# Window attention and a displaced blur on one core: who issues the stores of the residual and of the output, and in how many pieces the residual is read back

## The reference, cut to what matters

```python
x = x + window_attention(group_norm(x))   # 7x7 windows, 12 heads of 16, relative bias, projection
x = x + blur(group_norm(x))               # each channel shifted by a whole offset, then a 5x5 Gauss
```

## Time and profile before

| | |
|---|---|
| median of 3 runs | 5955.9 us (5952.99 to 5961.64) |
| the profiled execution's own time | 5947.59 us |
| its span | 5945.8 us |
| TensorE matmuls busy | 5372.8 us (90% of the span) |
| VectorE busy | 4278.6 us (72%) |
| ScalarE busy | 3798.7 us (64%) |
| GpSimd busy | 3556.2 us (60%) |
| mean granted TensorE clock | 0.936 |

### The profile page before, as it was taken

How to read it: one execution, slowest core, us unless ns; L and a number is a source line. 1 busy time by engine, 2 the same in 40 slices (tenths; PEclk the granted TensorE clock), 3 DMA queues, 4 the chain that set the end, 5 groups by cost and what they waited for, 6 DMA issues and landing times.

```text
span 5945.8 us, 259453 instructions
## 1 busy us (share of the span) xinstructions
PE 5372.8 (90%) x98232; PEld 4462.4 (75%) x98232; DVE 4278.6 (72%) x9682; ACT 3798.7 (64%) x8451; POOL 3556.2 (60%) x3940
## 2 busy tenths in 40 slices
PE   4998999999999999999999999999999999999996
PEld 3777777777777777777777777777777777777775
DVE  3777777777777777777777777777777777777773
ACT  1666666666666666667666666666666666666662
POOL 0566556666566666566665566665666655566664
PEclk9999999999999999999999999999999999999996
DMA  2566665666665666655666655666656666656653
GB/s 60 128 139 143 141 139 129 135 138 143 138 138 124 143 136 144 142 133 126 143 137 141 142 132 130 141 139 136 145 125 134 138 141 139 139 128 136 137 129 65
DMA packets 1353356, 790.32 MB, mean 133 GB/s; under 512 B 1187912, under 2 KB 1237512, under 8 KB 1344392
## 3 DMA queue, kind: packets, MB, share of 16 engines
q1 hardware_dynamic: 1352200, 774.03, 58.6%
HBM read 157.09 MB, written 154.14 MB: 52 GB/s over the span
## 4 chain that ended last, share of the span: by engine, by line
PE 37%; SPq 33%; issue 10%; ACT 8%; DVE 6%; DMA 5%; POOL 0%; ACTq 0%; DVEq 0%; POOLq 0%
SPq L414 13%; SPq L420 11%; PE pO L641 6%; SPq L432 5%; PE pT L624 3%; DMA xr<-x_scratch 2%; PE pS L598 2%; PE pS L590 2%; PE pM L509 2%; PE pT L617 2%; PE pT L608 2%; PE pM L511 2%; PE pM L510 1%; PE pO L651 1%; DMA kst<-mix 1%
## 5 line engine op out<-in xcount | busy, mean ns | idle before, releaser
L1222 POOL TENSOR_TENSOR probl<-prob,probh 98x588 f16<-98x588 f32 x1024 | 1332.2, 1301 | 398.3 <-DVE probh L1066 287.8
L1228 POOL TENSOR_TENSOR o<-osb,o 128x192 f16<-128x192 f32 x1024 | 598.6, 585 | 1434.0 <-ACT o L860 1414.9
L641 PEld LDWEIGHTS pO<-vv,probh 98*49 98x49 f16 x24576 | 866.2, 121 | 206.7 <-issue 151.6
L641 PE MATMUL pO<-vv,probh 98*49 98x34 f16 x24576 | 1017.7, 225 | 1.4 <-ACT om L868 1.2
L641 PE MATMUL pO<-vv,probl 98*49 98x34 f16 x12288 | 990.0, 228 | 2.3 <-issue 2.3
L852 ACT ACTIVATE mov<-pT 12x98 f16<-12x98 f32 x1024 | 244.6, 239 | 993.9 <-PE pT L608 992.7
L1051 DVE TENSOR_REDUCE mx<-pS 128x12 f32<-128x588 f32 x1024 | 776.7, 759 | 18.9 <-PE pS L598 6.1
L641 PEld LDWEIGHTS pO<-vv,probl 98*49 98x49 f16 x12288 | 765.9, 121 | 2.4 <-issue 2.4
L847 ACT ACTIVATE prob<-pT 98x588 f32<-98x588 f32 x1024 | 671.7, 656 | 147.0 <-PE pT L624 133.0
L624 PE MATMUL pT<-qst,kst 96*98 96x49 f16 x12288 | 750.8, 207 | 1.0 <-issue 0.8
L590 PE MATMUL pS<-biasT,addb 128*64 128x294 f16 x4096 | 617.5, 310 | 124.9 <-DMA kst<-mix 77.7
(11 more groups left out here) (192 smaller groups left out, 16086.5 us busy)
## 6 DMA issues: line engine op xcount, KB each, us to landing
kst<-kh SPq DMA_DIRECT2D x1536, 98.0 KB, 2.2
qst<-qh SPq DMA_DIRECT2D x1536, 49.0 KB, 2.4
qst<-mix SPq DMA_DIRECT2D x768, 98.0 KB, 2.6
kst<-mix SPq DMA_DIRECT2D x768, 98.0 KB, 2.5
vv<-cv SPq DMA_DIRECT2D x1024, 73.5 KB
xr<-x_scratch SPq DMA_DIRECT2D x64, 1176.0 KB
out<-xr SPq DMA_DIRECT2D x256, 294.0 KB
x_scratch<-xm SPq DMA_DIRECT2D x256, 196.0 KB, 3.2
```

What stands on the lines that cost most here:

```text
L641: mm = pe.matmul(pO[64 * win:64 * win + NT, OW * hp:OW * hp + OW], b[0:98, p % 2, PW * hp + NT * win:PW * hp + NT * win + NT], vv[:, g % 2 ...
L1222: pool.tensor_tensor(probl[0:98, p % 2, :], prob[0:98, p % 2, :], probh[0:98, p % 2, :], ALU.subtract).then_inc(S["pl_p"], 1)
L1228: pool.tensor_tensor(o16[:, p % 2, C:2 * C], osb[:, p % 2, :], o16[:, p % 2, 0:C], ALU.subtract).then_inc(S["ol_p"], 1)
```

## The change

The stores leave SP and go to ACT, where they stand behind the exponential of a step, two transfers in a step: chunk 0 of x1 at steps 16 and 17, chunk 1 at 24 and 25, chunk 2 at 0 and 1, chunk 3 at 6 and 7 of the next body (first the two from `xm`, then the two from `xt`); the output's quarters at 19, 23, 27 and 31 as before. The stores of chunk 3 count on a semaphore of their own. SP reads the residual back in four transfers of 24 channel places each, over all 112 partitions (588 KB each), at steps 6, 10, 12 and 14, and GpSimd waits for one quarter before every fourth multiplication. Before the first store of a new image, at step 16, ACT waits for all four quarters.

```diff
+READS = (6, 10, 12, 14)
...
-            def read_x1(s):
-
-                sp.dma_start(xr[HW * s:HW * s + HW, :],
-                             scratch[s].rearrange("y c x -> y (c x)")).then_inc(S["xr_in"], 16)
+            def read_x1(i, n):
+
+                cols = slice(CC // 4 * n, CC // 4 * n + CC // 4)
+                sp.dma_start(xr[0:SY, CC // 4 * HW * n:CC // 4 * HW * (n + 1)],
+                             scratch[:, :, cols].rearrange("s y c x -> (s y) (c x)")).then_inc(S[f"xr_in{n}"], 16)
...
-                    if p % PPC == PPC - 1 and p > PPC and att:
-                        store_x1(i, p // PPC - 1)
-                    if p == 5 and prev:
-                        store_x1(i - 1, NCH - 1)
                     if p == 6 and prev:
 
+                        sp.wait_ge(S["x1_last"], nth("x1_last", i, 0))
                         sp.wait_ge(S["x1_out"], nth("x1_out", i, 0))
                         if due("y_out", i - 1, 0):
                             sp.wait_ge(S["y_out"], nth("y_out", i - 1, 0))
-                        read_x1(0)
-                    if p == 8 and prev:
-                        read_x1(1)
+                        read_x1(i - 1, 0)
+                    if p in READS[1:] and prev:
+                        read_x1(i - 1, READS.index(p))
...
-                    b = blur_step(p, 16, prev)
-                    if b is not None and b % 4 == 3:
-
-                        sp.wait_ge(S["y_dve"], nth("y_dve", i - 1, b + 1))
-                        c = slice(b // 4 * CPP, b // 4 * CPP + CPP)
-                        v = out[(i - 1).row()].rearrange("(c s) y x -> s y c x", s=2)
-                        for s in (0, 1):
-                            src = xr[HW * s:HW * s + HW, :].rearrange("y (c x) -> y c x", x=HW)
-                            sp.dma_start(v[s][:, c], src[:, c]).then_inc(S["y_out"], 16)
...
+            def store_x1(i, k, tail):
+
+                done = S["x1_last" if k == NCH - 1 else "x1_out"]
+                t, h = slice(CHUNK * k, CHUNK * k + CHUNK), k // 2
+                act.wait_ge(S["x1_p"], nth("x1_p", i, 4 * k + 4))
+                y = slice(2 * WS * k, 2 * WS * k + 2 * WS)
+                for s in (0, 1):
+                    if tail:
+                        act.dma_start(scratch[s, y, CM // 2:CC].rearrange("y c x -> c y x"),
+                                      xt[64 * h + s:64 * h + 64:2, par(i), CHUNK * (k % 2):CHUNK * (k % 2) + CHUNK]
+                                      .rearrange("c (y x) -> c y x", x=HW)).then_inc(done, 16)
+                    else:
+                        act.dma_start(scratch[s, y, 0:CM // 2].rearrange("y c x -> c y x"),
+                                      xm[s::2, par(i), t].rearrange("c (y x) -> c y x", x=HW)).then_inc(done, 16)
+
+            def store_out(i, b):
+
+                act.wait_ge(S["y_dve"], nth("y_dve", i, b + 1))
+                c = slice(b // 4 * CPP, b // 4 * CPP + CPP)
+                v = out[i.row()].rearrange("(c s) y x -> s y c x", s=2)
+                for s in (0, 1):
+                    src = xr[HW * s:HW * s + HW, :].rearrange("y (c x) -> y c x", x=HW)
+                    act.dma_start(v[s][:, c], src[:, c]).then_inc(S["y_out"], 16)
+
+            def stores(i, p, prev, att):
+
+                if p == 2 * PPC and prev and att:
+                    for n in range(4):
+                        act.wait_ge(S[f"xr_in{n}"], nth(f"xr_in{n}", i - 1, 16))
+                k, late = divmod(p - 2 * PPC, PPC)
+                if att and 0 <= k and late < 2:
+                    store_x1(i, k, late)
+                if prev and p < 2:
+                    store_x1(i - 1, NCH - 2, p)
+                if prev and p in (6, 7):
+                    store_x1(i - 1, NCH - 1, p - 6)
+                b = blur_step(p, 16, prev)
+                if b is not None and b % 4 == 3:
+                    store_out(i - 1, b)
+
             def body(i, prev, att, nxt):
                 for p in range(PAIRS):
                     for n, q in at(p, 1, prev, att, nxt):
                         exp(i + n, q)
+                    stores(i, p, prev, att)
                     for n, q in at(p, 3, prev, att, nxt):
                         out_hi(i + n, q)
...
                         if b == 0:
-                            pool.wait_ge(S["xr_in"], nth("xr_in", i - 1, 32))
                             pool.wait_ge(S["gn2_dve"], nth("gn2_dve", i - 1, 13))
+                        if b % (NB // 4) == 0:
+                            name = f"xr_in{b // (NB // 4)}"
+                            pool.wait_ge(S[name], nth(name, i - 1, 16))
```

More of the change, by code:

```diff
@@ L227, in build @@
             "const_in", "setup", "setup_act", "setup_pe",
-            "x_in0", "x_in", "x1_out", "xr_in", "y_out", "stack_q", "stack_k", "stack_t", "vst0", "vst1",
+            "x_in0", "x_in", "x1_out", "x1_last", "xr_in0", "xr_in1", "xr_in2", "xr_in3", "y_out", "stack_q", "stack_k", "stack_t", "vst0", "vst1",
             "gn1_bn", "gn2_bn", "gn1_dve", "gn1_pe", "gn1_pool", "gn2_dve", "gn2_pe", "gn2_pool",
@@ L235, in build @@
             "c1_pe", "z_act", "z_dve", "c2_pe", "y_dve")}
-        PER = {"x_in0": 16, "x_in": 48, "x1_out": 256, "xr_in": 32, "y_out": 8 * 16, "stack_q": 192 * NCH,
+        PER = {"x_in0": 16, "x_in": 48, "x1_out": 192, "x1_last": 64, "xr_in0": 16, "xr_in1": 16, "xr_in2": 16, "xr_in3": 16, "y_out": 8 * 16, "stack_q": 192 * NCH,
                "stack_k": 192 * NCH, "stack_t": 192 * NCH, "gn1_bn": 12, "gn2_bn": 12, "gn1_dve": 8, "gn1_pe": 2, "gn1_pool": 2,
```

## The result

The changed kernel takes 5697.9 us (median of four runs, 5678.74 to 5705.81); the kernel before, run beside it, 5954.4 us. The ratio is 0.9564, with a 95% interval of 0.9537 to 0.9591. I had forecast 5831 us and a range of 5730 to 6000: right in sign, wrong in size, and outside the range. The time is that of the rival "all of it goes", though not by its terms, as the part on the prediction shows. The profiled execution took 5705.81 us with a span of 5704.0, 241.8 us under the span before.

A forecast was written before the change was run, and what follows sets the result against it. It took TensorE's waits tied to transfers (198.4 us) and the lower clock behind them as the bound. 70 + 75 + 45 - 65 = 125 us less gave 5823 profiled, 5831 us predicted; range 5730 to 6000, 8 times in 10.

The forecast's parts named there:

- all of it goes: Rival: stack wait 78, stalls 121, clock 100 all gone, ACT costing only 40; 259 us less, 5697 us; chance 0.12.
- A, stack wait: TensorE's wait before L590 for stacked keys, 77.7 us: SP freed of stores starts chunk 1's first lot earlier, 70 us gained.
- the row is under 20, as listed: Sign named beforehand: TensorE's wait row at L590 for the stacked keys falls under 20 us.
- B, issue stalls: TensorE's stalls before L598 (90.4 us) and L617 (30.3), read as instruction fetches behind big transfers: smaller reads gain 75 us.
- L598's part: Stall before L598, 90.4 us in 28 times: half, 45 us, taken as gained, since the next fetch may be hit.
- three quarters of the bytes to three quarters of the time: Batch before L598's stall falls from 2352 to 1764 KB, so it was taken to shorten by about 3 us.
- C, clock: Slow stretches behind the two waits in steps 6 to 11 return to full clock: 45 us gained of at most 162.
- D, ACT's issues: Issuing stores on ACT delays its compute: 65 us lost, between 12 (issues running beneath the exponential) and 85; upper bound 384.
- full price: Each pair of ACT's issues costs its whole length less ACT's reserve: 2.8 us a body, 85 us over 30 bodies.
- The stall did not only move: Rival: TensorE arrives earlier, still finds the fetch missing or another lot late; about 5950 us (5925 to 5975), chance 0.14.
- ACT does not wait for the fourth quarter: Rival: ACT waits 3.8 us at step 16 for the residual's last quarter; 140 us slower, 6096 us, chance 0.12.
- SP's and ACT's issues do not exclude each other: Last rival: each ACT issue waits 0.6 us for one of SP's; 254 us slower, 6210 us, chance 0.08.

## Why the prediction was right in sign and wrong in size

**A, stack wait: right.** I took 70 us, 61.0 went (77.7 to 16.7); SP begins 0.02 us behind its data, and the row is under 20, as listed. The run with the stores alone (15.9) shows that it is their doing, and the run with the output on SP (25.8) that of the two it is mainly the residual's, and not the output's last quarter that my rows showed ahead of the lot.

**B, issue stalls: right mechanism, too little.** I took 75, 96.0 went (123.8 to 27.8). I took only half of L598's part, because the smaller batch might hit the next fetch; of its 90.4 us, 75.1 went, and 10.2 came back before L618. The runs with halves show what I missed: the quarters are also spread over 112 partitions instead of 56, and that alone took 60.1 us of stalls (107.7 to 47.6) with the bytes unchanged. My step from three quarters of the bytes to three quarters of the time was the wrong one: the quarter that I estimated at 6.2 us lands in 4.9 (median). That "issue" is a missing fetch, which I had argued from one stretch, the trace of the kernel before bears out. Of its 45 issue stalls of over 1 us, 40 contain the end of an instruction packet (queue q8), TensorE goes on 1.55 us behind it (median), and that packet starts 11.7 us after the one before it, where the median over the span is 6.7. The one at the stall of the earlier trace rows starts at 2312.69.

**C, clock: mis-sized.** I took 45 of at most 162, and TensorE's busy time fell by 76.4. "A bit over a quarter" had no row behind it, and the price, half of a stretch's length, was too high. Low time is span x (1 - clock) x 2, 5945.8 x 0.064 x 2 = 761 us before and 5704.0 x 0.042 x 2 = 479 after. Laid over TensorE's busy time in the trace, 632 us of it before and 411 after fall on matmuls, 220 less. Half of that would be 110, so a low us over matmuls cost 0.35 us here and not 0.5. Against the changed kernel, the run with the stores alone gives 0.43 by the same working (107 us more low time over matmuls, 45.6 more busy), the two with 56 waits 0.44 and 0.36. The clock is 0.958, and in steps 6 to 11 it is 1.00 in the body shown and 0.96 on the mean.

**D, ACT's issues: mis-sized, by TensorE's waits the largest miss.** I took 65, nearer the full price of 85 than the 12 of issues beneath the exponential. By TensorE's waits it is 21: `o` 17.6 and `mov` 3.6 more. By the mean steps it is 1.3 us a body, 40 us: 0.7 each in steps 0 and 1 (1.4 where I said 1.6), less 0.4 that steps 2 to 5 give back, and 0.3 in steps 16 to 31, where my terms make 1.2. The step that failed is the reason I gave, that the row I had was for an engine that does nothing else. An issue runs beside an ACTIVATE on the same engine: of 559 us of issues ACT stood still for 270, and moving them ahead of the exponential costs the 37 us that this hides. By the mean steps, 1.0 of that run's 1.2 us a body are in steps 16 to 31. In steps 0 and 1 my full price came nearly true, though the overlap is there too, because a pair is longer there, 1.9 and 1.8 us on the mean against the 1.5 that I took and 1.3 in steps 16 and 17.

**Small waits: not in the sum.** VectorE's `mx` 46.5 to 30.6, `xc` 13.3 to 4.1, `pjt` 5.7 to 0.7, `cv` 9.3 to 4.4: 35 us that went with the rest, and that I had no term for.

Against the sum of -125 the terms (D by the waits) miss by +9 (A), -21 (B), -31 (C), -44 (D) and some -30 (small waits, less the 4.4 that the two views leave open), which makes the -242 measured. Four of five err to the same side, which is why the range failed too: I had left most of the rival "all of it goes" out of it as if its terms were independent. That its 5697 is the time measured is luck: its stack wait (78) measured 61, its stalls (121) 96, its clock (100) 76 and its ACT (40) 21, and the small waits, which it left out too, filled the gap.

**The other rivals.** The stall did not only move, but what is left of it did: on the mean of bodies 2 to 29 the issue stalls were 4.0 us a body in steps 10 to 12, and are 0.9 in steps 6, 9 and 10. ACT does not wait for the fourth quarter: SP issues it at step 15, at 2259.15, it lands at 2263.6, before the first store at 2265.68, and ACT's rows have no wait for a transfer. The reserve is small: over all bodies the fourth quarter lands 0.2 to 5.0 us ahead of that store. SP's and ACT's issues do not exclude each other. Issues of ACT (min/median/max in ns):

```profile
L870 ACTq DMA_DIRECT2D x_scratch<-xt x256: 616/624/2243, 226.8 to 5624.2; - x128
L884 ACTq DMA_DIRECT2D out<-xr x256: 326/550/2847, 393.8 to 5698.4; - x128
```

The median is SP's 0.65, not 1.2, although 473 of the 512 issues of the residual overlap one of SP's, and SP's lot took 8.69 against 8.33 undisturbed. Some single issues are long (the pairs of 2.06 and 2.67 us above, at the start of the body); what holds those is not shown. The last rival would have shown as 0.6 us more on each. Its rule, that the sequencer locks a shared descriptor generator for exclusive use, stands in the Trainium skill in "Perfetto Trace Analysis", section "DMA Instruction — HWDGE (DVE, Sync)"; these runs show no such cost in the median.

**Left open.** Why the clock falls in steps 13 and 14, where TensorE has no wait of note: 6 to 9 us at the lower clock there in every kernel but the one with the loads at step 9, which has 2.5 and stood still long before, at step 10. Why a read into half of the partitions takes longer, and whether fewer DMA engines and longer rows do it together. Which single transfer holds an instruction fetch.

## What to carry to other kernels

When an engine only issues, look at how late it is against its data, and move just the issues that make it late: here the residual's stores, while the output's brought nothing. Price a wait of the busiest engine as the wait plus 0.35 to 0.45 of the low-clock time that falls on its work behind it, and let terms that hang on one another (a wait, the clock behind it, the small waits after that) go all together in the range's lower end. If a big transfer can be spread over all partitions instead of half, do that before cutting it into pieces.

## What the runs showed of the hardware that was not expected

A DMA issue on ACT runs beside the ACTIVATE ahead of it: issued 0.24 us into a 0.66 us exponential, and ACT's idle time for 559 us of issues was 270. ACT's transfers go in a queue of their own (q10, 154.19 MB). A read of 1176 KB took 7.6 us into 112 partitions; one of 1344 KB took 10.2 into 64 and one of 1008 KB 13.1 into 48. TensorE went on 1.55 us (median) after the end of a late instruction packet. Adding 56 instructions to a body of TensorE cost 5 to 6 us at another place of it, where a second instruction packet now comes in one step, nearly as much as the stand-still that they made.
